# Attention over graph edges on one core: the edge networks' steps in another order, and one wait less on GpSimd

## The chip, the cores and the metric

One core of a Trainium2 chip. The number given is the device time of one execution in microseconds (us). Engines are called TensorE (PE in the profile, its weight loads PEld), VectorE (DVE), ScalarE (ACT), GpSimd (POOL) and SyncE (SP).

## The reference

A graph with 6250 nodes of 64 features and 206,250 edges sorted by their first node runs through two layers: a relation layer (gather, gate, segment sum, tanh) and an attention layer. The kernel's stages follow them; the change is in the attention layer's pass over the edges:

```python
W_k = lin(ssp(lin(edge_attr, wkn_w1, wkn_b1)), wkn_w2, wkn_b2)   # edge network, 32 -> 16 -> 16
keys_j = lin(W_k[:, None, :] * h_keys[col], wkl_w, wkl_b)        # 4 heads of 16
qk_ij = jnp.sum(queries_i * keys_j, axis=-1)
alpha = segment_softmax(qk_ij, row, n)
W_v = lin(ssp(lin(edge_attr, wvn_w1, wvn_b1)), wvn_w2, wvn_b2)   # the second edge network
msg_j = lin(W_v[:, None, :] * h_values[col], wvl_w, wvl_b)
aggr = jax.ops.segment_sum(alpha[:, :, None] * msg_j, row, num_segments=n)
```

with `ssp(x) = softplus(x) - log 2`. All of it is in float32.

## The kernel before

`attention_layer` (line 1313 on) handles the sorted edges as 128 runs, one for each partition, of 1612 edges, in 62 chunks of T = 26 edges a partition. The loop helper emits the first pair of chunks, a hardware loop over the 29 between, and the last pair; in each body b = 0, 1 is the chunk of the pair and n = 2i + b its number. Each engine has its own written-out order, and they meet at semaphores alone. A wait is passed when its semaphore has reached a count, so `wait_ge(s_w, n + 1)` is "chunk n's turned weights are there".

For one chunk n:

- SyncE loads the chunk's edge records (`attr`, line 1376) and query starts (`qin`, line 1378), two buffers each.
- VectorE's `index` writes the chunk's node numbers as integers (`idx`, line 1518) and where a new first node starts (`same`, line 1526). It stands at the head of the turn before, so `s_idx` for n comes when VectorE enters turn n - 1.
- GpSimd issues 26 indirect DMAs (line 1395), each of which gathers one row of keys and values (512 bytes) for every partition into `got[b]`. Before the first of them it waits for `s_used` (the buffer's last user, chunk n - 2), `s_idx`, and `s_w` >= n, that is for chunk n - 1's turned weights.
- The edge networks, for both `W_k` and `W_v` at once: ScalarE packs the attributes (`flat_attr`, line 1448); TensorE transposes them in 7 groups, two halves of 4 and 3, into bank `p_a` (line 1411); ScalarE copies them out (`attr_t`, line 1452); TensorE's first product goes to `p_z` (line 1416); ScalarE takes Relu and the absolute value (lines 1456 and 1457), an exponential and a logarithm (lines 1459 and 1460), which make the softplus; VectorE's `activated` adds the two parts (line 1530); TensorE's second product goes to `p_a` again (line 1420), half by half, the second after the copy of the first; ScalarE adds the bias (`net_t`, line 1467, in `networks_end`); TensorE turns the result back to edges on partitions (`p_w`, line 1424), after VectorE is through with the chunk before's (`s_value`).
- VectorE's `chunk`: a scan that carries each query along its run (line 1537, after ScalarE's `marks`, line 1442), then, with `p_w` and the gathered rows there, `prod` (line 1545), a product with the network's weights (1548), a sum by head (1549), the running maximum (1557), `drop` and `below` (1560 to 1563), the value product (1567, `s_value`); it waits for ScalarE's exponentials (lines 1472 to 1475, `s_exp`), multiplies them in (`add_a`, line 1572, `s_used`) and scans the state (line 1580, `s_state`).
- ScalarE turns the state for the store and issues it (lines 1483 and 1486).

In one turn n ScalarE does: query n+1 laid out, the whole network of chunk n+1 up to the logarithm, then `finish(n)`: exponentials of n, `networks_end(n+1)`, the copy of the maxima, then with the state there `marks(n+1)`, the copy of the state and the store. VectorE's `activated(n+1)` stands between the value product and the wait for the exponentials.

In the stage before and the ones after, other indirect DMAs run: `sort` (line 625, scatters) and `attention_nodes` (line 1696, 49 gathers in a row); their rows are used too.

Of the kernel before, what the change touches and what calls it, by code (L numbers as in the profile page):

```python
# [22 lines left out]
P = 128  # L23
# [8 lines left out]
CHUNKS = NT // T  # L32
# [4 lines left out]
G = 4  # L37
# [1275 lines left out]
def attention_layer(k):  # L1313
# [4 lines left out]
    with ExitStack() as ctx:  # L1318
# [31 lines left out]
        p_a, p_z = bank("p_a"), bank("p_z")  # L1350
# [10 lines left out]
        records_v, starts_v, sums_v = by_run(k.records), by_run(k.q_starts), by_run(k.sums1)  # L1361

        halves = ((0, 4 * P, 4), (4 * P, GROUPS * P, GROUPS - 4))

        with nc.Block() as block:
# [20 lines left out]
            def _(pool):  # L1386
                def body(i):
                    for b in range(2):
# [3 lines left out]
                        wait(pool, s_w, n)  # L1392
# [8 lines left out]
            @block.tensor  # L1401
            def _(pe):
                def body(i):
                    for b in range(2):
                        n = 2 * i + b
                        pe.wait_ge(s_flat, n + 1)
                        for j, (c0, c1, groups) in enumerate(halves):
                            wait(pe, s_at_copied, 2 * n + j)
                            wait(pe, s_net_copied, 2 * n)
                            for g in range(c0 // P, c0 // P + groups):  # L1410
                                last = nc.tensor.transpose(p_a[:, g * P - c0:(g + 1) * P - c0], flat_attr[:, g * G:(g + 1) * G, :].rearrange("p t c -> p (t c)"), k.ident[:])  # L1411
                            last.then_inc(s_at, 1)
                        for j, (c0, c1, groups) in enumerate(halves):
                            pe.wait_ge(s_at_copied, 2 * n + j + 1)
                            wait(pe, s_z_read, 2 * n + j)
                            nc.tensor.matmul(p_z[:, 0:c1 - c0], k.w1_t[:], attr_t[:, c0:c1], start=True, stop=True).then_inc(s_z, 1)
                        pe.wait_ge(s_ssp, n + 1)
                        for j, (c0, c1, groups) in enumerate(halves):
                            wait(pe, s_net_copied, 2 * n + j)
                            nc.tensor.matmul(p_a[:, 0:c1 - c0], k.w2_t[:], relu[:, c0:c1], start=True, stop=True).then_inc(s_net, 1)  # L1420
                        wait(pe, s_value, n)
                        pe.wait_ge(s_net_copied, 2 * n + 2)
                        for g in range(GROUPS):
                            last = nc.tensor.transpose(p_w[:, g * P:(g + 1) * P], net_t[:, g * P:(g + 1) * P], k.ident[:])
                        last.then_inc(s_w, 1)

                loop(pe, body)

            @block.scalar
            def _(act):  # L1430
# [13 lines left out]
                def networks(n, i, b):  # L1444
# [3 lines left out]
                    nc.scalar.copy(flat_attr[:, 0:T, :], attr[b][:, :, 0:EC]).then_inc(s_flat, 1)  # L1448
                    wait(act, s_z, 2 * n)
                    for j, (c0, c1, _) in enumerate(halves):  # L1450
                        act.wait_ge(s_at, 2 * n + j + 1)
                        nc.scalar.copy(attr_t[:, c0:c1], p_a[:, 0:c1 - c0]).then_inc(s_at_copied, 1)
                    wait(act, s_net, 2 * n)
                    for j, (c0, c1, _) in enumerate(halves):
                        act.wait_ge(s_z, 2 * n + j + 1)
                        nc.scalar.activation(relu[:, c0:c1], p_z[:, 0:c1 - c0], ACT.Relu, bias=k.b1_c[:])
                        nc.scalar.activation(soft[:, c0:c1], p_z[:, 0:c1 - c0], ACT.Abs, bias=k.b1_c[:]).then_inc(s_z_read, 1)
# [4 lines left out]
                def networks_end(n):  # L1462

                    wait(act, s_w, n)
                    for j, (c0, c1, _) in enumerate(halves):
                        act.wait_ge(s_net, 2 * n + j + 1)
                        nc.scalar.activation(net_t[:, c0:c1], p_a[:, 0:c1 - c0], ACT.Identity, bias=k.b2_c[:]).then_inc(s_net_copied, 1)

                def finish(n, i, b):
# [6 lines left out]
                    if not at_end(i, b):  # L1476
                        networks_end(n + 1)
# [513 lines left out]
```

## Time and profile before

| | |
|---|---|
| median of 3 runs | 5864.14 us (5855.48 to 5867.09) |
| the profiled execution | 5865.56 us |
| its span | 5863.7 us |
| attention layer's loop, first to last `prod` | 3436.7 to 5692.3 us |
| GpSimd, VectorE, ScalarE, TensorE busy over the span | 56%, 66%, 47%, 46% |

The page gives for each engine its busy time and share of the span, then 40 slices, the DMA queues, the chain that ended last, and groups of instructions by line. The order of time (timeline) has for each instruction its start, its length, and in brackets how long the engine had stood still before it and what ended that. "issue" there means that the engine waited for nothing that the profile shows, "remote" that a semaphore came whose sender isn't resolved. Ends of TensorE's matmuls are modelled; starts are records.

### The profile page before, as it was taken

The page shows a single profiled execution, that of the slowest core. Times are in us where ns is not written, and L with a number is a line of the kernel's source. Part 1 is how long each engine was busy: PE and PEld are TensorE (multiplying, and loading weights), DVE is VectorE, ACT ScalarE, POOL GpSimd, SP SyncE. Part 2 cuts the span into 40 slices and gives each one's busy share as a digit, 9 for nine tenths or more (in the row PEclk, how much of TensorE's full clock was granted, in tenths as well). Part 3 has the DMA queues.
Part 4 walks back from the last instruction along what each step waited for, and adds up shares of the span by engine and source line. Part 5 has one row for each costly group of instructions (what it writes and reads, how often), then busy time and mean ns, then how long its engine had stood idle before and what let it go on. Part 6 is the DMA issues. An engine that isn't in the chain of part 4 may idle for free. (4 is left out here: it accounts for less than half of the span.)

```text
span 5863.7 us, 79660 instructions
## 1 busy us (share of the span) xinstructions
PE 2726.4 (46%) x21110; PEld 1693.1 (29%) x21111; DVE 3881.4 (66%) x8751; ACT 2758.0 (47%) x5413; POOL 3278.9 (56%) x3388
## 2 busy tenths in 40 slices
PE   7655555555555555555488622322223222222223
PEld 7433333333333333333388511111111111111102
DVE  9867777777777777776599645655556666655552
ACT  3244444444444444444122345655555555555552
POOL 0146565666666565656610266666666666666653
PEclk8555555555555555555577755555555555555555
DMA  5112121212121212121477533433334343433321
GB/s 64 55 54 71 63 71 62 71 63 71 63 71 63 71 63 71 63 71 58 103 160 145 72 103 100 124 110 108 108 103 111 109 110 103 110 108 109 109 79 24
DMA packets 691304, 505.28 MB, mean 86 GB/s; under 512 B 588446, under 2 KB 605214, under 8 KB 691109
## 3 DMA queue, kind: packets, MB, share of 16 engines
q1 hardware_dynamic: 573012, 246.99, 18.2%
q0 software_dynamic: 108736, 196.93, 11.6%
q10 hardware_dynamic: 9360, 59.56, 2.7%
q14 instruction: 172, 1.40, 0.1%
q8 instruction: 24, 0.39, 0.0%
HBM read 289.96 MB, written 213.26 MB: 86 GB/s over the span
## 5 line engine op out<-in xcount | busy, mean ns | idle before, releaser
L625 POOL DMA_INDIRECT records<-rec,place x1612 | 1557.2, 966 | 1306.9 <-issue 451.0
L1395 POOL DMA_INDIRECT got_a<-kv_table,idx_a x1612 | 1539.5, 955 | 762.8 <-issue 691.9
L860 DVE SCALAR_TENSOR_TENSOR same_before<-p_src,src_f,before 128x128 bf16<-128x128 f32 x1612 | 775.0, 535 | 0.0
L711 ACT ACTIVATE lo_away<-p_lo,minus_number 128x512 bf16<-128x512 f32 x434 | 291.2, 671 | 615.5 <-remote 593.6
L668 PE MATMUL p_src<-fields,select 3*128 3x512 bf16 x434 | 248.3, 572 | 687.7 <-DVE same_before L860 512.0
L1411 PE MATMUL p_a<-ident,flat_attr 128*128 128x128 f32 x434 | 123.5, 433 | 930.5 <-issue 447.4
L807 DVE TENSOR_TENSOR picked<-p_look,hi_hot 128x392 f32<-128x392 f32 x434 | 231.5, 533 | 407.5 <-remote 398.2
L1420 PE MATMUL p_a<-relu,w_t 128*128 128x512 f32 x248 | 230.8, 1034 | 463.4 <-issue 332.5
L850 DVE TENSOR_SCALAR dst_hot<-p_dst,number 128x512 bf16<-128x512 f32 x434 | 307.3, 708 | 191.1 <-remote 178.1
L643 PE MATMUL p_look<-table_low,lo_hot_t 128*128 128x98 bf16 x1612 | 410.2, 281 | 0.0
L643 PE MATMUL p_look<-table_rest,lo_hot_t 128*128 128x98 bf16 x1612 | 409.4, 280 | 0.0
L1545 DVE TENSOR_TENSOR prod<-got_a,wide 128x1664 f32<-128x1664 f32 x62 | 117.0, 1888 | 440.2 <-remote 216.3
L643 PE MATMUL p_look<-table,lo_hot_t 128*128 128x98 bf16 x1612 | 402.3, 278 | 0.0
L730 ACT ACTIVATE h_gated<-p_h,gate_s 128x64 f32<-128x64 f32 x1586 | 372.1, 315 | 51.5 <-remote 12.2
L653 PE MATMUL p_h<-window,dst_hot 128*128 128x64 bf16 x4836 | 357.6, 242 | 65.1 <-issue 64.9
L1014 PE MATMUL acc<-high,lo_r 128*128 128x64 bf16 x1708 | 345.4, 244 | 60.0 <-DVE low L1079 40.7
L708 ACT COPY table<-p_place 128x49 f32<-128x49 f32 x434 | 91.7, 211 | 597.0 <-issue 371.6
L1411 PEld LDWEIGHTS p_a<-ident,flat_attr 128*128 128x128 f32 x434 | 75.6, 215 | 978.3 <-issue 824.4
L1014 PE MATMUL acc<-rest_r,lo_r 128*128 128x64 bf16 x1708 | 344.3, 243 | 0.0
L1014 PE MATMUL acc<-low,lo_r 128*128 128x64 bf16 x1708 | 344.2, 243 | 0.0
L653 PEld LDWEIGHTS p_h<-window,dst_hot 128*128 128x128 bf16 x4836 | 312.2, 133 | 54.2 <-issue 53.8
L1014 PEld LDWEIGHTS acc<-high,lo_r 128*128 128x128 bf16 x1708 | 291.3, 171 | 67.6 <-issue 66.3
(377 smaller groups left out, 8443.3 us busy)
## 6 DMA issues: line engine op xcount, KB each, us to landing
sums<-packed_a ACTq DMA_DIRECT2D x62, 936.0 KB
q_starts<-zero_q SPq DMA_DIRECT2D x62, 884.0 KB
rec_r<-records SPq DMA_DIRECT2D x124, 442.0 KB
qin<-q_starts SPq DMA_DIRECT2D x62, 884.0 KB
attr_a<-records SPq DMA_DIRECT2D x62, 442.0 KB
records<-rec,place POOLq DMA_INDIRECT x1612
got_a<-kv_table,idx_a POOLq DMA_INDIRECT x1612
stage<-in_edge_attr SPq DMA_DIRECT2D x61, 416.0 KB
```

Of the source, the lines that this page charges most:

```text
L625: nc.gpsimd.indirect_dma_start(k.records, bass.IndirectOffsetOnAxis(ap=place[b][:, t:t + 1], axis=0), rec[b][:, t, :], None).then_inc(s_se ...
L643: last = nc.tensor.matmul(p_look[qb][:, j * 2 * HI:(j + 1) * 2 * HI], lo_hot_t[qb][:, j * P:(j + 1) * P], part, start=(e == 0), stop=(e == 2))
L653: last = nc.tensor.matmul(p_h[qb][:, j * D:(j + 1) * D], dst_hot[qb][:, j * P:(j + 1) * P], part, start=(e == 0), stop=(e == 2))
L668: nc.tensor.matmul(p_src[:, 0:m * P], k.select[:, NODE, :], rows, start=True, stop=True).then_inc(s_src, 1)
L711: nc.scalar.activation(lo_away[qb][:, 0:m * P], p_lo[:, 0:m * P], ACT.Abs, bias=k.minus_number[:]).then_inc(s_lo_away, 1)
L730: last = nc.scalar.activation(to, p_h[qb][:, j * D:(j + 1) * D], ACT.Copy, scale=gate[b][:, t:t + 1])
L807: v.tensor_tensor(picked[:, 0:n, :, :], p_look[gb][:, 0:n * 2 * HI].rearrange("p (g a h) -> p g a h", a=2, h=HI), bc(group_hot(k, b, g, HI ...
L850: v.tensor_scalar(dst_hot[qb][:, 0:m * P], p_dst[:, 0:m * P], k.number[:], None, ALU.is_equal).then_inc(s_dst_hot, 1)
L860: last = v.scalar_tensor_tensor(same_before[:, first:first + j + 1, :].rearrange("p g e -> p (g e)"), p_src[:, 0:(j + 1) * P], k.src_f[:, ...
L1014: last = nc.tensor.matmul(acc[:, to(t // SUPER)], lo[b][:, :, t], part, start=False, stop=True, skip_group_check=True)
L1395: nc.gpsimd.indirect_dma_start(got[b][:, t, :], None, k.kv_table, bass.IndirectOffsetOnAxis(ap=idx[b][:, t:t + 1], axis=0)).then_inc(s_got ...
L1420: nc.tensor.matmul(p_a[:, 0:c1 - c0], k.w2_t[:], relu[:, c0:c1], start=True, stop=True).then_inc(s_net, 1)
```

## The change

Only `attention_layer` is touched.

- GpSimd: the wait for `s_w` goes; `s_used` and `s_idx` stay.
- PSUM: instead of `p_a` (transposed attributes, second product) and `p_z` (first product) there are `p_n[0]` and `p_n[1]`, one for each half, used by all three in turn.
- TensorE, in turn n: second product of chunk n+1, transposes of chunk n+2, turned weights of n+1, first product of n+2.
- ScalarE, in turn n: lay out the query n+1, `networks_end(n+1)`, `flattened(n+2)`, exponentials of n, `attributes(n+2)`; then with the state of n there `marks(n+1)`, `activation(n+2)`, the maxima's and the state's copies, the store.
- VectorE: `activated(n+1)` moves ahead, between the query scan and `prod` of turn n, and is made of seven additions of 128 columns, one for each group, instead of one of 896.
- Before the loop, networks 0 and 1 are begun.

```diff
-        p_a, p_z = bank("p_a"), bank("p_z")
+        p_n = [bank(f"p_n{j}") for j in range(2)]
...
+        def follows(i, b, more):
+
+            return not (isinstance(i, int) and 2 * i + b + more >= CHUNKS)
...
                         wait(pool, s_used, n - 1)
                         pool.wait_ge(s_idx, n + 1)
-                        wait(pool, s_w, n)
                         pool.sem_inc(k.s_passed, 1)
...
+                def attributes(m):
+                    pe.wait_ge(s_flat, m + 1)
+                    wait(pe, s_net_copied, 2 * m)
+                    for j, (c0, c1, groups) in enumerate(halves):
+                        for g in range(c0 // P, c0 // P + groups):
+                            last = nc.tensor.transpose(p_n[j][:, g * P - c0:(g + 1) * P - c0], flat_attr[:, g * G:(g + 1) * G, :].rearrange("p t c -> p (t c)"), k.ident[:])
+                        last.then_inc(s_at, 1)
+
+                def first_product(m):
+                    for j, (c0, c1, groups) in enumerate(halves):
+                        pe.wait_ge(s_at_copied, 2 * m + j + 1)
+                        nc.tensor.matmul(p_n[j][:, 0:c1 - c0], k.w1_t[:], attr_t[:, c0:c1], start=True, stop=True).then_inc(s_z, 1)
+
+                def second_product(m):
+                    for j, (c0, c1, groups) in enumerate(halves):
+                        pe.wait_ge(s_ssp, 2 * m + j + 1)
+                        pe.wait_ge(s_z_read, 2 * m + j + 1)
+                        nc.tensor.matmul(p_n[j][:, 0:c1 - c0], k.w2_t[:], relu[:, c0:c1], start=True, stop=True).then_inc(s_net, 1)
+
+                def turned(m):
+                    wait(pe, s_value, m)
+                    pe.wait_ge(s_net_copied, 2 * m + 2)
+                    for g in range(GROUPS):
+                        last = nc.tensor.transpose(p_w[:, g * P:(g + 1) * P], net_t[:, g * P:(g + 1) * P], k.ident[:])
+                    last.then_inc(s_w, 1)
+
+                attributes(0)
+                first_product(0)
+                second_product(0)
+                attributes(1)
+                turned(0)
+                first_product(1)
+
                 def body(i):
                     for b in range(2):
                         n = 2 * i + b
...
+                        if follows(i, b, 1):
+                            second_product(n + 1)
+                        if follows(i, b, 2):
+                            attributes(n + 2)
+                        if follows(i, b, 1):
+                            turned(n + 1)
+                        if follows(i, b, 2):
+                            first_product(n + 2)
...
-                def finish(n, i, b):
+                def exponentials(n):
 
                     act.wait_ge(s_below, n + 1)
                     nc.scalar.activation(add[:, D:QW, 1:T1], below[:], ACT.Exp)
                     nc.scalar.activation(weight, below[:], ACT.Exp)
                     nc.scalar.activation(factor[:, 0:D, :].rearrange("p (h d) t -> p h d t", h=NH), bc(drop[:], 2, HD), ACT.Exp)
                     nc.scalar.activation(factor[:, D:QW, :], drop[:], ACT.Exp).then_inc(s_exp, 1)
-                    if not at_end(i, b):
-                        networks_end(n + 1)
+
+                def finish(n, i, b):
+
+                    act.wait_ge(s_state, n + 1)
+                    if follows(i, b, 1):
+                        marks(n + 1, i + b, 1 - b)
+                    if follows(i, b, 2):
+                        activation(n + 2)
                     wait(act, s_store[b], 16 * i)
                     c.mark(nc.scalar.copy(packed[b][:, :, QW:SW], top[b][:, :, 1:T1].rearrange("p h t -> p t h")))
-                    act.wait_ge(s_state, n + 1)
-                    if not at_end(i, b):
-                        marks(n + 1, i + b, 1 - b)
...
-                        if not at_end(i, b):
+                        if follows(i, b, 1):
                             lay_out(n + 1, i + b, 1 - b)
-                            networks(n + 1, i + b, 1 - b)
+                            networks_end(n + 1)
+                        if follows(i, b, 2):
+                            flattened(n + 2, i + 1, b)
+                        exponentials(n)
+                        if follows(i, b, 2):
+                            attributes(n + 2)
                         finish(n, i, b)
...
                 def activated(n):
                     dve.wait_ge(s_soft, n + 1)
-                    nc.vector.tensor_tensor(relu[:], relu[:], soft[:], ALU.add).then_inc(s_ssp, 1)
+                    for j, (c0, c1, groups) in enumerate(halves):
+                        for g in range(groups):
+                            at = slice(c0 + g * P, c0 + (g + 1) * P)
+                            last = nc.vector.tensor_tensor(relu[:, at], relu[:, at], soft[:, at], ALU.add)
+                        last.then_inc(s_ssp, 1)
...
                     c.then(nc.vector.tensor_copy(query[1 - b][:, :, 0:1], factor[:, :, T:T1]))
 
+                    if follows(i, b, 1):
+                        activated(n + 1)
                     dve.wait_ge(s_w, n + 1)
                     dve.wait_ge(s_got[b], SCATTERED * (i + 1))
```

## Rows read from the trace of the kernel before

**Rows 1.** The page, busy us, share of the span and instructions by engine

```profile
PE 2726.4 (46%) x21110; PEld 1693.1 (29%) x21111; DVE 3881.4 (66%) x8751; ACT 2758.0 (47%) x5413; POOL 3278.9 (56%) x3388
```

**Rows 2.** The source line 1545: durations in ns (least, median, most), first and last start

```profile
L1545 DVE TENSOR_TENSOR prod<-got_a,wide x62: 1886/1887/1890, 3436.7 to 5692.3; 128x1664 f32<-128x1664 f32 x62
```

**Rows 3.** Busy time by stretch: window, us, PE, PEld, DVE, ACT, POOL, clock, DMA

```profile
3450.00:5600.00 2150.00, 629.54 (x1282) 269.01 (x1282) 1281.49 (x1220) 1223.97 (x1232) 1438.76 (x1507) 0.50 0.39 108
```

**Rows 4.** Groups by line, 3450 to 5600 us: busy us, mean ns, idle before

```profile
L1395 POOL DMA_INDIRECT got_a<-kv_table,idx_a x1507 | 1439.2, 955 | 711.5 <-issue 660.8 <-remote 34.0 <-DVE idx_a L1518 16.7
L1537 DVE TENSOR_TENSOR_SCAN wide<-wide,query 128x1836 f32<-128x1836 f32 x58 | 231.4, 3990 | 50.6 <-issue 43.4 <-ACT wide L1442 7.3
...
L1474 ACT ACTIVATE wide<-drop 128x1728 f32<-128x1728 f32 x59 | 96.3, 1633 | 0.0
L1442 ACT COPY wide<-same 128x1768 f32<-128x1768 f32 x58 | 94.9, 1636 | 216.7 <-DVE state_a L1580 216.7
...
L1472 ACT ACT_TABLE_LOAD x59 | 75.7, 1283 | 1.0
```

**Rows 5.** Order of time, 4500 to 4625 us: start, length, instruction, idle before

```profile
4506.47 1.92 PE L1416 MATMUL p_z<-attr_t,w_t 128*128 128x512 f32 x2
...
4511.83 0.69 ACT L1456 ACTIVATE relu<-p_z,b_c 128x512 f32<-128x512 f32 x1 [4.63 <-issue]
...
4521.11 1.09 DVE L1530 TENSOR_TENSOR relu<-relu,soft 128x896 f32<-128x896 f32 x1 [3.74 <-ACT soft L1460]
4521.54 1.47 POOL L1395 DMA_INDIRECT got_a<-kv_table,idx_a  x1 [0.30 <-issue]
...
4528.67 1.73 PE L1424 MATMUL p_w<-ident,net_t 128*128 128x128 f32 x7 [1.78 <-issue]
...
4532.35 0.18 DVE L1518 CAST idx_a<-attr_a 128x26 int32<-128x26 f32 x1 [0.61 <-DVE state_a L1580]
...
4537.07 0.95 POOL L1395 DMA_INDIRECT got_a<-kv_table,idx_a  x1 [0.30 <-issue]
...
4542.42 1.09 PE L1411 MATMUL p_a<-ident,flat_attr 128*128 128x128 f32 x4 [12.03 <-ACT flat_attr L1448]
...
4546.28 0.59 ACT L1452 COPY attr_t<-p_a 128x512 f32<-128x512 f32 x1 [4.10 <-remote]
4546.37 1.89 DVE L1545 TENSOR_TENSOR prod<-got_a,wide 128x1664 f32<-128x1664 f32 x1 [8.47 <-remote]
...
4546.95 0.95 POOL L1395 DMA_INDIRECT got_a<-kv_table,idx_a  x1 [8.93 <-issue]
...
4553.61 0.27 DVE L1563 TENSOR_TENSOR below_a<-logit_carry,top 128x104 f32<-128x104 f32 x1
...
4560.61 2.99 DVE L1572 TENSOR_TENSOR add_a<-got_a,wide 128x1664 f32<-128x1664 f32 x1 [2.42 <-issue]
...
4563.65 1.73 PE L1424 MATMUL p_w<-ident,net_t 128*128 128x128 f32 x7 [0.77 <-ACT net_t L1467]
...
4621.07 0.94 POOL L1395 DMA_INDIRECT got_a<-kv_table,idx_a  x1 [8.89 <-issue]
```

**Rows 6.** Order of time in the last stage, 5733 to 5806 us

```profile
5733.21 0.96 POOL L1696 DMA_INDIRECT sums_f<-sums,last_at  x1 [2.04 <-DMA sums<-fixed,fix_to]
...
5756.31 0.69 DVE L1843 TENSOR_TENSOR xs<-xs,out_br 128x512 f32<-128x512 f32 x1 [8.91 <-remote]
...
5773.77 2.08 PE L1719 MATMUL p_of<-out_t,feat_f 128*128 128x128 f32 x8 [5.31 <-issue]
...
5794.18 0.94 POOL L1696 DMA_INDIRECT sums_f<-sums,last_at  x1 [0.30 <-issue]
...
5801.86 0.69 DVE L1843 TENSOR_TENSOR xs<-xs,out_br 128x512 f32<-128x512 f32 x1 [40.06 <-remote]
```

**Rows 7.** Order of time in the first stage's sort, 343 to 349 us

```profile
343.25 0.96 POOL L625 DMA_INDIRECT records<-rec,place  x1 [0.30 <-issue]
...
348.40 0.57 DVE L807 TENSOR_TENSOR picked<-p_look,hi_hot 128x392 f32<-128x392 f32 x1 [23.92 <-remote]
```

More of the change, by code:

```diff
@@ L1405, in body @@
                         n = 2 * i + b
[L1406 to L1425, printed above, removed]
+                        if follows(i, b, 1):
[6 more added lines that the diff above has]
+                            first_product(n + 2)
                 loop(pe, body)
@@ L1442, in marks, with flattened @@
                     nc.scalar.copy(factor[:, :, 1:T1], bc(same[b][:], 1, QW)).then_inc(s_keep, 1)
-                def networks(n, i, b):
+                def flattened(n, i, b):
                     act.wait_ge(s_rec[b], 16 * (i + 1))
@@ L1448, in networks, with attributes @@
                     nc.scalar.copy(flat_attr[:, 0:T, :], attr[b][:, :, 0:EC]).then_inc(s_flat, 1)
+                def attributes(n):
                     wait(act, s_z, 2 * n)
@@ L1451, in networks, with activation @@
                         act.wait_ge(s_at, 2 * n + j + 1)
-                        nc.scalar.copy(attr_t[:, c0:c1], p_a[:, 0:c1 - c0]).then_inc(s_at_copied, 1)
+                        nc.scalar.copy(attr_t[:, c0:c1], p_n[j][:, 0:c1 - c0]).then_inc(s_at_copied, 1)
+                def activation(n):
                     wait(act, s_net, 2 * n)
@@ L1466, in networks_end @@
                         act.wait_ge(s_net, 2 * n + j + 1)
-                        nc.scalar.activation(net_t[:, c0:c1], p_a[:, 0:c1 - c0], ACT.Identity, bias=k.b2_c[:]).then_inc(s_net_copied, 1)
-                def finish(n, i, b):
+                        nc.scalar.activation(net_t[:, c0:c1], p_n[j][:, 0:c1 - c0], ACT.Identity, bias=k.b2_c[:]).then_inc(s_net_copied, 1)
+                def exponentials(n):
                     act.wait_ge(s_below, n + 1)
@@ L1491, in _ @@
                 lay_out(0, 0, 0)
-                networks(0, 0, 0)
+                flattened(0, 0, 0)
+                attributes(0)
+                activation(0)
                 networks_end(0)
+                flattened(1, 0, 1)
+                attributes(1)
+                activation(1)
                 def body(i):
@@ L1567, in chunk @@
                     nc.vector.tensor_tensor(by_head, by_head, bc(nets[:, :, HD:EC], 2, NH), ALU.mult).then_inc(s_value, 1)
-                    if not at_end(i, b):
-                        activated(n + 1)
                     dve.wait_ge(s_exp, n + 1)
```

4 lines of the change are left out of this document (2 added, 2 removed).

## The prediction, made before the change was built or run

> **What bounds the kernel now.** I read the totals of engines first [rows 1]: no engine is busy more than 66% of the span, so the limit has to be looked for by stage. The stage that the change touches is the attention layer; its first and last `prod` lie at 3436.7 and 5692.3 us [rows 2], that is 2255.6 us for 61 steps, 36.98 us a chunk. In the stretch 3450 to 5600 GpSimd is busiest with 67%, VectorE has 60%, ScalarE 57% [rows 3]. By lines [rows 4], GpSimd does one thing there, the indirect DMA of line 1395, 955 ns each; the row "0.30 <-issue" behind most of them in the order of time [rows 5] says that back to back they start every 1.25 us, so 26 take 32.5 us. GpSimd therefore stands still 4.5 us a chunk, and it does so in one piece: [rows 5] shows the gap of 8.93 us that ends at 4546.95 and the next one, of 8.89 us, that ends at 4621.07. 74.12 us apart, two chunks: 2 x 32.5 + 8.9 + some tenths. That gap is what the stage is over GpSimd's own time.
>
> What ends it? Burst n waits for `s_used`, `s_idx` and `s_w` >= n (the turned weights of chunk n-1). Before the gap ending at 4546.95, the index was written at 4532.35 + 0.18, and the seven transposes of line 1424 are modelled as ended at 4528.67 + 1.73 = 4530.4. The last indirect DMA started at 4537.07. Still nothing moved until 4546.3: then ScalarE's copy of `p_a` ("<-remote"), VectorE's `prod` and GpSimd's next burst all started within 0.7 us, although the copy waits only for transposes modelled as ended at 4543.51 [rows 5]. What the three have in common is TensorE. So I read it so: TensorE's completions came late, at about 4546.2, 15.8 us after the modelled end and 8.2 us after GpSimd's last issue ended (4538.0). In the other chunk of each pair the transposes at 4563.65 held nobody up. The page shows the same twice elsewhere. In the last stage GpSimd issues 49 indirect DMAs in a row from 5733.21 to 5795.1; products modelled as ended at 5775.85 are followed by VectorE only at 5801.86, 26 us later and 6.7 us after the last issue ended; earlier in that run VectorE had waited 8.91 us until 5756.31 for the same kind of product ("remote") [rows 6]. In the first stage VectorE waits 23.92 us for `p_look`, until 348.40, which is 4.2 us after a run of 26 ended at 344.2 [rows 7]. 26, 49 and 52 issues in a row, and a release 4.2, 6.7 and 8.2 us after the last: about 0.16 us for each issue. Early in a run (1 to 27 in this stage) completions come on time; `p_z` of 4506.47 + 1.92 at about the 28th issue is read at 4511.83, 3.4 us late [rows 5]. The Trainium skill ("Perfetto Trace Analysis", Tensor Engine Instruction) says that the profiler's end of a TensorE instruction is computed and not observed, and that the semaphore comes when PSUM acknowledges; the trace agrees (26 us between the two above).
>
> **The change, part by part.** (1) *No `s_w` wait on GpSimd*: 62 waits less. GpSimd is then stopped only by `s_used` (chunk n-2) and `s_idx` n, both written when VectorE enters turn n-1. That wait was what stopped GpSimd while TensorE's completion was outstanding, and its stop was what let the completion through. The gap of 8.9 us per pair goes if nothing else stops GpSimd.
> (2) *Networks up to two chunks ahead*: the same transposes, products and activations are issued, in another order. `turned(n+1)` now follows the value product of chunk n, some 9.3 us after `prod` began (4546.37 to the end of `below` at 4553.88, and then one product of 1.9 us), so it has some 23 us until `prod` n+1 instead of none; `attributes`, `first_product` and `second_product` have 6 to 13 us each before ScalarE blocks on them. This absorbs the 1 to 5 us of lateness at issues 28 to 44, not 15 and more. The queue behind them: ScalarE's `networks_end(n+1)` waits for the second product and stands in front of `exponentials(n)`; VectorE's `add_a`, its state scan, and with them `s_used` and the next index, wait behind that.
> (3) *A bank for each half*: the wait of the second product for the first copy (0.9 us, hidden) goes: 0.
> (4) *Exponentials at once*: `below` ends at 4553.61 + 0.27, `add_a` starts at 4560.61 because line 1460 and its table load stood in front [rows 5]. Now a table load (1.28 us) and 2.2 us of exponentials (1.63 the widest, three small ones [rows 4]): `add_a` 3.2 to 4.5 us earlier. VectorE's turn becomes prod to state 17 to 18.3 us, marks 1.7, scan and copy 4.4 [rows 4], `activated` 1.1 to 2, some 26 us, under GpSimd's 32.5. No gain of its own.
> (5) *Seven adds of 128 for one of 896*: 1.09 us becomes at most 7 x 0.27 = 1.9 (the 128x104 operations take 0.27 [rows 5]), hidden by (4). GpSimd's issue at 4521.54 took 1.47 instead of 0.95 beside this add [rows 5]; were each chunk's stretch saved, 62 x 0.5 = 31 us at most, 0 at least; about 12 if one in two and a half. Only counted where GpSimd bounds.
> (6) *Record and query loads, the store*: the record load of chunk n+2 is released by VectorE's `same` of chunk n and is read over 30 us later; a load is there some 5 us after its issue. On SP's and ScalarE's queues nothing new blocks: 0. The second network before the loop costs ScalarE some 9 us, behind the 32 us of the first burst: 0 to 3.
>
> **The sum.** What is decisive is what TensorE's completions do when GpSimd is not stopped for them. Taking from [rows 5, 6, 7] that after some 45 issues in a row a completion waits until GpSimd stops: VectorE and ScalarE go on until `networks_end` lacks its product; by then the indices of two further bursts are written, so GpSimd issues three bursts, 97.5 us, before it stops. Release: between 8.2 us (as now) and 0.16 x 78 = 12.5 us after. Then `networks_end` 1.2, `flattened` 0.9, table 1.3, exponentials 2.2, `add_a` 3.0, copy 0.2, scan 4.0, index 0.8 = 13.6 us until the next burst. 119.3 to 123.6 us for three chunks, 39.8 to 41.2 a chunk; I take 40.5. Against 36.98 that is +3.5 x 59 chunks (the first and last two run freer) = +207. If the held step is `first_product`, 13 us of activation and `activated` come in addition: 45 a chunk, +480. 5865.56 (span 5863.7 and 1.9 around it) + 207 = 6072; the profiled run lies 1.4 over the median, so 6071.
>
> **Rivals.** *GpSimd runs free* (0.26): completions late by a few us only, inside the new slack. For it: issues 1 to 44, where the lateness is 0 to 5 us, and in the last stage one completion came at the 19th issue without a stop. Then 32.6 to 32.8 a chunk, 4.3 less x 61 = -262: 5603. The Trainium skill ("SBUF — State Buffer", SBUF: two separate sides) says that only VectorE and GpSimd share a port and that TensorE never waits on anyone at SBUF; by it this rival would be the forecast, and [rows 6, 7] speak against it.
> *Partly held* (0.12): completions trickle through at 5 to 10 us each, and the slack takes most of it: 34 to 36 a chunk, 5685 to 5805.
> *The hidden queue fills* (0.08): 52 issues and 8.2 us of draining are 1.41 us an issue; if GpSimd is slowed to that, 26 take 36.7 us, 0.3 x 61 less than now: 5847. Half of it, with some late completions, falls within the 0.2% (12 us, about what a measurement of this kernel can tell from no change).
> *The change doesn't do what it says* is in the second: if ScalarE's blocked waits keep the networks from running ahead.
>
> **Chances.** Forecast (held until GpSimd stops) 0.54; 5603: 0.26; 5685 to 5805: 0.12; 5847: 0.08. Slower by over 0.2% 0.54, within 0.2% 0.05, faster 0.41. The forecast's own range is 5990 to 6300. The range reaches from the free case, 5595, to 6300; above it lies part of the 45 us case.
>
> **What would show it.** Right: GpSimd in runs of 78 issues or more, gaps of 20 us and over between them, ended by index or `add_a`; ScalarE's line of `networks_end` or `attributes` waiting 15 us and more for TensorE. Wrong: GpSimd without a gap over 1 us for many chunks and `prod` every 32.6 us. Exponentials right behind `below` confirm (4), and no issue over 1.1 us beside the adds (5). Wrong by size if runs end after 52 because VectorE is blocked a chunk earlier.

## The result and the profile after

The changed kernel takes 6196.84 us (median of 4 runs, 6185.89 to 6204.86) against 5863.1 (4 runs, 5855.48 to 5867.09) of the kernel before: a ratio of 1.057, interval 1.0553 to 1.0586. Forecast were 6071, range 5595 to 6300.

The page of the changed kernel, busy time by engine over a span of 6184.1 us (against [rows 1]):

```profile
PE 2660.0 (43%) x21110; PEld 1717.2 (28%) x21111; DVE 3904.3 (63%) x9123; ACT 2736.3 (44%) x5413; POOL 3259.4 (53%) x3388
```

Every engine is busy for as long as before, within 2.5%, and all shares fell: the 320.4 us by which the span grew are waiting. The source lines of the product by factor (`prod`) and of GpSimd's gathers (durations in ns: least, median, most; then first and last start), against [rows 2, 4]:

```profile
L1594 DVE TENSOR_TENSOR prod<-got_a,wide x62: 1872/1880/1889, 3436.1 to 6012.9; 128x1664 f32<-128x1664 f32 x62
...
L1398 POOL DMA_INDIRECT got_a<-kv_table,idx_a x1612: 938/944/1092, 3393.9 to 6005.2; - x180
...
  DVE idx_a L1561: 607.0, 29
  issue: 491.2, 1578
```

The first product starts where it did (3436.1, before 3436.7), the last one 171.2 us before the end of the span (before 171.4). Between them lie 2576.8 us, 42.24 a chunk against 36.98 [rows 2]; 5.26 x 61 = 321 us, which is the whole loss. GpSimd waits 607 us for the index, in 29 waits, 20 of them over 25 us long; [rows 4] had 16.7 us of that kind. Counted from the starts of its issues, it falls into a cycle of exactly three chunks: 52 issues, a break of 0.9 to 1.7 us, 26 issues, then nothing for close to 30 us, and that every 127.6 us, 42.5 a chunk. The waits of one stretch, 3450 to 5900 us (engine, line and what it waited for: us, times, longest):

```profile
ACT relu L1486 <- remote: 694.1, 72, 22.5
DVE relu L1576 <- ACT soft L1490: 659.0, 42, 28.8
POOL got_a L1398 <- DVE idx_a L1561: 565.8, 27, 29.7
```

They are one chain: ScalarE waits for TensorE, VectorE for ScalarE, GpSimd for VectorE. One instance of it in the order of time, 4345 to 4410 us (against [rows 5]):

```profile
4345.50 2.07 PE L1417 MATMUL p_n<-attr_t,w_t 128*128 128x512 f32 x2 [6.29 <-issue]
...
4353.29 0.48 ACT L1479 COPY attr_t<-p_n 128x384 f32<-128x384 f32 x1 [7.84 <-remote]
...
4353.82 1.65 PE L1417 MATMUL p_n<-attr_t,w_t 128*128 128x384 f32 x2 [6.24 <-issue]
...
4377.14 0.69 ACT L1486 ACTIVATE relu<-p_n,b_c 128x512 f32<-128x512 f32 x1 [21.84 <-remote]
...
4377.91 0.94 POOL L1398 DMA_INDIRECT got_a<-kv_table,idx_a  x1 [0.30 <-issue]
4379.16 0.94 POOL L1398 DMA_INDIRECT got_a<-kv_table,idx_a  x1 [0.30 <-issue]
...
4383.39 0.58 ACT L1486 ACTIVATE relu<-p_n,b_c 128x384 f32<-128x384 f32 x1 [4.98 <-remote]
...
4387.80 1.50 DVE L1576 TENSOR_TENSOR relu<-relu,soft 128x128 f32<-128x128 f32 x7 [28.08 <-ACT soft L1490]
...
4389.23 1.88 DVE L1594 TENSOR_TENSOR prod<-got_a,wide 128x1664 f32<-128x1664 f32 x1
...
4401.44 3.00 DVE L1619 TENSOR_TENSOR add_a<-got_a,wide 128x1664 f32<-128x1664 f32 x1 [2.92 <-ACT wide L1505]
...
4404.61 3.98 DVE L1627 TENSOR_TENSOR_SCAN state_a<-wide,add_a 128x1836 f32<-128x1836 f32 x1
...
4408.80 0.18 DVE L1561 CAST idx_a<-attr_a 128x26 int32<-128x26 f32 x1 [0.20 <-DVE state_a L1627]
...
4409.76 0.94 POOL L1398 DMA_INDIRECT got_a<-kv_table,idx_a  x1 [29.66 <-DVE idx_a L1561]
```

The two halves of the first product are modelled as ended at 4347.57 and 4355.47. ScalarE gets the first at 4377.14 and the second at 4383.39, 29.6 and 27.9 us later; the second comes 3.3 us after GpSimd's 78th issue has ended (4380.10). From there 26.4 us of dependent work lead to GpSimd's next issue.

The first half came at 4377.14 while GpSimd was still issuing (its next issues start at 4377.91 and 4379.16), and this is the rule in this trace, not the exception. I set each recorded increment of a semaphore by TensorE against the modelled end of the instruction that made it. Between 3450 and 5900 us, 328 of 401 left a record; 146 of them came more than 2 us late, the latest 33.0 us, and 124 of these 146 came in the middle of a run of issues. The late ones come in the order in which they were made; 94 times two of them follow each other inside a run, 40 times 4.9 us apart and never less. What was made while GpSimd stood still mostly came at once in this trace: 4 of 136 were over 2 us late, against 142 of the 192 made during a run. In the kernel before (3450 to 5600 us), 66 of 258 came more than 2 us late, up to 16.5 us, and 47 of these 66 after the run.

### The profile page after: what moved, and what is told of

Same layout as the page of the kernel before. It is cut to its first block and busy times, and to the rows that moved or that the text cites. A ratio compares the mean times of both kernels' runs of the same rounds, so it can differ in the third digit from the quotient of the medians.

```text
span 6184.1 us, 79942 instructions
## 1 busy us (share of the span) xinstructions
PE 2660.0 (43%) x21110; PEld 1717.2 (28%) x21111; DVE 3904.3 (63%) x9123; ACT 2736.3 (44%) x5413; POOL 3259.4 (53%) x3388
## 5 line engine op out<-in xcount | busy, mean ns | idle before, releaser
L1398 POOL DMA_INDIRECT got_a<-kv_table,idx_a x1612 | 1524.1, 945 | 1099.7 <-DVE idx_a L1561 607.0
L1423 PE MATMUL p_n<-relu,w_t 128*128 128x512 f32 x248 | 207.4, 992 | 1380.3 <-DVE relu L1576 844.3
L1576 DVE TENSOR_TENSOR relu<-relu,soft 128x128 f32<-128x128 f32 x434 | 93.6, 286 | 853.0 <-ACT soft L1490 734.2
L1423 PEld LDWEIGHTS p_n<-relu,w_t 128*128 128x128 f32 x248 | 72.9, 324 | 1507.4 <-DVE relu L1576 901.3
L1486 ACT ACTIVATE relu<-p_n,b_c 128x512 f32<-128x512 f32 x124 | 78.4, 633 | 758.2 <-remote 739.3
L1584 DVE TENSOR_TENSOR_SCAN wide<-wide,query 128x1836 f32<-128x1836 f32 x62 | 247.4, 3990 | 186.7 <-issue 162.2
```

The costliest lines, as they stand in the source:

```text
L1398: nc.gpsimd.indirect_dma_start(got[b][:, t, :], None, k.kv_table, bass.IndirectOffsetOnAxis(ap=idx[b][:, t:t + 1], axis=0)).then_inc(s_got ...
L1423: nc.tensor.matmul(p_n[j][:, 0:c1 - c0], k.w2_t[:], relu[:, c0:c1], start=True, stop=True).then_inc(s_net, 1)
L1584: nc.vector.tensor_tensor_scan(flat, flat, query[b][:].rearrange("p c t -> p (c t)"), 0.0, ALU.mult, ALU.add).then_inc(s_q, 1)
```

## The experiments

Four groups of runs landed on four chips. The kernel before was timed on each again, and it isn't the same there: 5868.03 us on the chip of E1 to E4, 5028.36 (E5 to E8), 5026.85 (E9, E10) and 5027.06 (E12; one run of 5025.04 beside E11). I call the first a chip that holds TensorE's results, that is, on which the other engines get them late, and the others chips that don't; the traces below show the difference, not its reason. Whether it belongs to the chip or to its condition at the time was not tested. The expectations of E5 to E8 were written for a chip that holds.

### On the chip that holds

**E1**: the old order without GpSimd's wait for the turned weights.

```diff
                         pool.wait_ge(s_idx, n + 1)
-                        wait(pool, s_w, n)
                         pool.sem_inc(k.s_passed, 1)
```

> The kernel before with one line taken out: GpSimd no longer waits for the turned weights. Order of the networks, banks and exponentials are those of before. Theory held (TensorE's completions are held up while GpSimd issues indirect DMAs without a stop): runs of 78 issues; the turned weights of every third chunk are modelled as ended at about the 47th issue and are read only when the run of 78 is over; cycle 97.5 + 3.3 + 22 = 123 us for three chunks, 41.0 a chunk, 5863 + 4.0 x 59 = 6100 us (6040 to 6160). Rival order (the new order of steps is what costs, the wait on GpSimd was harmless): no slower than 5870, and down to 5600 if GpSimd was only being paced for nothing.

Measured: 6137.45 us, ratio 1.0464 (1.0391 to 1.0537). Product by factor, and GpSimd's line:

```profile
L1544 DVE TENSOR_TENSOR prod<-got_a,wide x62: 1886/1887/1890, 3454.2 to 5945.9; 128x1664 f32<-128x1664 f32 x62
...
L1394 POOL DMA_INDIRECT got_a<-kv_table,idx_a x1612: 938/944/1859, 3417.1 to 5914.6; - x180
...
  issue: 487.4, 1585
  DVE idx_a L1517: 472.5, 27
```

2491.7 / 61 = 40.85 us a chunk, with runs of 78 and of 52 and 26 issues. So the removed wait alone does most of the damage, in the old order too: 3.87 of the 5.26 us a chunk.

**E2**: the changed kernel with another wait for GpSimd in that place.

```diff
                         pool.wait_ge(s_idx, n + 1)
+                        pool.wait_ge(s_z, 2 * n + 2)
                         pool.sem_inc(k.s_passed, 1)
```

> The changed kernel with one wait added: before burst n GpSimd waits for both halves of the first product of chunk n (s_z), the step that is read 28 to 30 us late in the changed kernel. Theory held: GpSimd stops after 52 issues at most while a completion is outstanding, is released some 3 to 8 us later, and the time falls by most of the loss: 36 to 38.5 us a chunk, 5800 to 5960 us. Rival order (ScalarE's and VectorE's new order costs by itself): GpSimd wasn't the cause, an added wait can't help, 6190 us or more.

Measured: 5869.16 us, ratio 1.0011 (0.9976 to 1.0045):

```profile
L1595 DVE TENSOR_TENSOR prod<-got_a,wide x62: 1872/1880/1889, 3490.4 to 5722.5; 128x1664 f32<-128x1664 f32 x62
...
L1399 POOL DMA_INDIRECT got_a<-kv_table,idx_a x1612: 939/945/1092, 3454.0 to 5719.9; - x180
...
  issue: 472.7, 1551
  remote: 259.6, 41
```

2232.1 / 61 = 36.59 us a chunk: GpSimd stops every 26 or 52 issues, for 3.3 to 8.7 us (twice for 1.1), and the whole loss of pitch is gone (42.24 to 36.59; before 36.98). TensorE's results still come late (3500 to 5700 us: 161 of 303 by more than 2 us), but at most by 25.7 us, and GpSimd now stops for the ones it waits for. The stage starts late, though, since burst 0 now waits for network 0: GpSimd at 3454.0 instead of 3393.9, the first `prod` at 3490.4 instead of 3436.1 us. These 54 us eat up the 0.39 x 61 = 24 us that the pitch gains on the kernel before, which leaves the profiled execution (span 5893.1) 29 us longer than the kernel before's; it is one of the longer ones, and by medians the two are the same.

**E3 and E4**: the 26 gathers of a chunk become one plain DMA of GpSimd, in the new order and in the old one. The gather by node is left out, the bytes stay; the waits for the gathered rows count one DMA in place of 26.

```diff
-                        for t in range(T):
-                            nc.gpsimd.indirect_dma_start(
-                                got[b][:, t, :], None, k.kv_table,
-                                bass.IndirectOffsetOnAxis(ap=idx[b][:, t:t + 1], axis=0)).then_inc(s_got[b], 16)
+                        nc.gpsimd.dma_start(got[b][:], k.kv_table[bass.ds(i * 2 * T + b * T, P * T), :].rearrange("(p t) c -> p t c", t=T)).then_inc(s_got[b], 16)
```

> The changed kernel with the 26 gathers of a chunk replaced by one plain DMA of as many bytes from the same table, issued by GpSimd behind the same waits (the gathered rows are the wrong ones: the gather by node is left out; everything else is computed). Theory held: no run of issues, so no held completion; VectorE's turn of 26 to 29 us sets the pace, 27.5 a chunk: 6190 - 15 x 61 = 5275 us (5180 to 5400). Rival order: the pace stays at 37 us a chunk or over, 5860 us or more. Rival transfers (the gathered bytes, not the issues, hold TensorE up): late completions as before, 5800 to 6190.

> The same replacement in the kernel before (the gather by node is left out there too). Theory held: VectorE's turn with prod to state 21.4 us, marks 1.8, scan 4.3, index 1 sets the pace, if TensorE's chain is in time: 29 to 33 us a chunk, 5390 to 5620 us, slower than the changed order by 1 to 4 us a chunk, since the exponentials come later there. Rival order: faster than the changed order by 3 us a chunk or more.

Measured: E3 5329.67 us (ratio 0.9086, 0.9018 to 0.9155), E4 5633.63 (0.9605, 0.954 to 0.967). The product by factor of E3, then of E4:

```profile
L1591 DVE TENSOR_TENSOR prod<-got_a,wide x62: 1874/1879/1889, 3494.6 to 5181.1; 128x1664 f32<-128x1664 f32 x62
```

```profile
L1542 DVE TENSOR_TENSOR prod<-got_a,wide x62: 1886/1889/1889, 3454.5 to 5479.1; 128x1664 f32<-128x1664 f32 x62
```

27.65 us a chunk in the new order, 33.19 in the old. Without a run of issues nothing is held: on this same chip none of 418 recorded increments (E3, 3500 to 5150 us) and none of 409 (E4, 3500 to 5450 us) came later than 0.02 us after the modelled end. The bytes gathered for a chunk are the same and come in less time, so the bytes alone don't hold TensorE; the 26 issues, or their smaller packets (4096 bytes against 13,312), do. The new order is then 5.5 us a chunk the better one. So the order itself isn't slow; it is slow beside unbroken runs of issues. E4's time lies 14 us over the range expected for it, and the difference between the orders over the 1 to 4 us expected.

### On chips that don't hold

**E8**: the changed kernel with the removed wait put back (`wait(pool, s_w, n)`, the line that E1 takes out).

> The changed kernel with the wait that the change took from GpSimd put back: chunk n's issues wait for chunk n - 1's turned weights. In the new order those are made a chunk earlier, before chunk n - 2's products by factor, so the wait is met before GpSimd comes to it. Theory (the stop counts, not the wait as such): runs of 78 issues stay, 42 us per chunk, 6150 to 6210 us. Rival (taking the wait away was the whole damage, and with it back the new order is worth its 5.5 us per chunk or at least nothing lost): 5600 to 5870 us.

Measured: 4994.78 us against 5028.36, ratio 0.9934 (0.9917 to 0.9951). On this chip the premise of both expectations is missing. Product by factor and GpSimd's line:

```profile
L1595 DVE TENSOR_TENSOR prod<-got_a,wide x62: 1879/1888/1889, 2874.7 to 4859.9; 128x1664 f32<-128x1664 f32 x62
...
L1399 POOL DMA_INDIRECT got_a<-kv_table,idx_a x1612: 941/947/1085, 2839.5 to 4857.2; - x180
...
  issue: 487.5, 1599
  DVE idx_a L1562: 15.1, 13
```

GpSimd makes all 1612 issues without a break as long as 1 us, 32.54 us a chunk, and TensorE's results are read at once all the same. In the order of time:

```profile
4007.75 3.35 PE L1424 MATMUL p_n<-relu,w_t 128*128 128x512 f32 x4 [11.59 <-DVE relu L1577]
...
4015.09 1.89 DVE L1595 TENSOR_TENSOR prod<-got_a,wide 128x1664 f32<-128x1664 f32 x1 [6.79 <-DMA got_a<-kv_table,idx_a]
...
4022.24 0.27 DVE L1613 TENSOR_TENSOR below_a<-logit_carry,top 128x104 f32<-128x104 f32 x1
...
4022.54 0.29 ACT L1503 ACTIVATE add_a<-below_a 128x104 f32<-128x104 f32 x1 [4.78 <-DVE below_a L1613]
...
4024.77 3.02 DVE L1620 TENSOR_TENSOR add_a<-got_a,wide 128x1664 f32<-128x1664 f32 x1 [0.47 <-ACT wide L1506]
...
4028.21 3.98 DVE L1628 TENSOR_TENSOR_SCAN state_a<-wide,add_a 128x1836 f32<-128x1836 f32 x1
```

Everybody is ahead of GpSimd here, and VectorE waits for its data. By the same count of TensorE's increments as above, in E8, 2900 to 4800 us, none of 410 came more than 0.02 us late, and the same is true of every other trace of these three chips (E5 to E7 and E9 to E12, 401 to 408 increments each). The restored wait never stopped GpSimd in E8 (no row names `p_w`), so E8 stands for the changed kernel on this chip; the changed kernel itself was not timed on such a chip.

**E5**: the wait of E2, but only from chunk 2 on.

```diff
                         pool.wait_ge(s_idx, n + 1)
+                        if not at_start(i):
+                            pool.wait_ge(s_z, 2 * n + 2)
                         pool.sem_inc(k.s_passed, 1)
```

> The changed kernel with GpSimd waiting for chunk n's first products before chunk n's 26 issues, but only from chunk 2 on, so that the first two chunks' issues start as in the changed kernel (3393.9 us) and not 60 us later. The order of the networks is whole. Theory (long runs of issues hold TensorE's results back; a short stop lets them through): 36.6 us per chunk as with the wait from chunk 0 on, first product by factor near 3440 instead of 3490.4, so 5869 - 50 = 5820 us (5800 to 5850), which is below both kernels. Rival (the start is worth nothing, since chunk 2 then waits for what the start gained): 5860 to 5880.

Measured: 4995.37 us, ratio 0.9934 (0.9918 to 0.9951), 32.53 us a chunk. The wait costs nothing that can be seen where nothing is held (E8, with the other wait, has 32.54). What it gives on a holding chip stays an expectation (5820), made of E2's pitch and the changed kernel's start.

**E6 and E9**: a pause behind each chunk's issues that depends on nobody.

```diff
                         pool.wait_ge(s_idx, n + 1)
+                        wait(pool, s_pause, n)
                         pool.sem_inc(k.s_passed, 1)
...
                                 bass.IndirectOffsetOnAxis(ap=idx[b][:, t:t + 1], axis=0)).then_inc(s_got[b], 16)
+                        nc.gpsimd.memset(idle[:], 0.0).then_inc(s_pause, 1)
```

> The changed kernel with a memset of 4096 columns of a tile that nobody reads behind each chunk's 26 issues, and GpSimd waiting for its end before the next chunk's issues: from the 128-column and the one-column memsets of this trace (194 and 99 to 106 ns) an estimate of 3.1 us. The pause depends on nothing that another engine does; nothing that is computed changes. Theory (the run of issues as such holds TensorE's results, any stop of a few us lets them through): runs of 26 issues, 32.5 + 3.3 = 35.8 us per chunk, 3620 + 61 x 35.8 = 5804 us (5780 to 5860). Rival A (the wait on s_z helps because it orders GpSimd behind the networks, not because it stops it; a stop of its own gives nothing): 42.2 us per chunk or more, 6150 to 6300. Rival B (3 us is too short a stop): in between, 38 to 41 us per chunk, 5940 to 6120.

> The kernel of e6 once more (a memset of 4096 columns behind each chunk's 26 issues), on whatever chip it lands: on the chip of e5 to e8 nothing held TensorE's results back, and e6 could only show what the pause costs there, 36.5 us per chunk. If the kernel before takes about 5865 us on this chip (a chip that holds): the theory (the run of issues holds the results, and any stop lets them through) says 36.5 us per chunk, 3620 + 61 x 36.5 = 5846 us (5820 to 5890), with runs of 26; the rival (a stop of its own gives nothing, it has to be a wait on TensorE) says 6150 to 6400. If the kernel before takes about 5030 us, this is the run of e6 again: 5230 to 5245.

Measured: 5240.38 us (ratio 1.0422, 1.0404 to 1.0439) and 5237.21 (1.0418, 1.0401 to 1.0435). The memset took 3.53 us (estimated 3.1), the pitch is (5098.6 - 2871.9) / 61 = 36.50 us:

```profile
L1404 POOL MEMSET idle<- x62: 3525/3530/3539, 2868.7 to 5096.9; 128x4096 f32 x62
```

These show only the price of a stop where nothing is held: 4.0 us a chunk, one for one, so GpSimd is the bound there. Whether a stop of its own would free TensorE on a holding chip stays open.

**E7 and E10**: the same issues with 272 bytes a partition in place of 512, keys and values left out; the buffers are cleared once before the loop.

```diff
-                                got[b][:, t, :], None, k.kv_table,
+                                got[b][:, t, 0:QW], None, k.q_table,
```

> The changed kernel with the same 1612 issues in the same order, but each fetches 68 columns of the query table (272 bytes per partition) and not 128 of keys and values (512); the other 60 columns of the buffer are zero. Keys and values are left out of what is computed. It tells the issues from the bytes that they move. Theory (the issues hold TensorE's results): runs of 78 issues with stops near 29 us as in the changed kernel, 41.5 to 42.5 us per chunk, 6150 to 6210 us. Rival (the transferred bytes or the load on the DMA engines do it): the hold is gone or much shorter, 33 to 38 us per chunk, 5650 to 5950 us.

> The kernel of e7 once more (1612 issues of 272 bytes per partition in place of 512; keys and values left out). If this chip holds (kernel before about 5865 us): the theory (the issues do it, not the bytes) says runs of 78 issues and 41.5 to 42.5 us per chunk, 6150 to 6210 us; the rival (bytes do it) 33 to 38 us per chunk, 5650 to 5950. If it doesn't hold: 4985 to 5000 as in e7.

Measured: 4993.88 and 4990.06 us (ratios 0.9934, 0.9918 to 0.9951, and 0.9928, 0.9911 to 0.9944), 32.49 us a chunk in E7: halving the bytes gives 0.05 us a chunk against E8, so there it is the issue itself that costs 1.25 us. What the bytes of each issue add to the hold stays open for the same reason; E3 shows only that as many bytes without the issues don't hold.

**E11**: the kernel before, unchanged, for its trace.

> The kernel before, unchanged, for its profile on whatever chip this is. On a chip that doesn't hold TensorE's results back (about 5028 us): GpSimd's 26 issues per chunk are 32.5 us without a stop, so the theory (there GpSimd's issues are the bound of both kernels) expects 61 chunks at 32.5 to 33.2 us by the product by factor, and GpSimd stopped only by short waits for the turned weights, 0 to 0.7 us per chunk; the 33 us by which the changed order was faster there is then either those stops (0.5 us per chunk) or the start and the end of the stage. Rival: VectorE's chain is the bound there too, with GpSimd idle several us per chunk. On a chip that holds (about 5865 us): 36.9 us per chunk as in its first profile.

Measured: 5024.07 us. Product by factor, gathers and the wide add:

```profile
L1545 DVE TENSOR_TENSOR prod<-got_a,wide x62: 1886/1887/1890, 2872.4 to 4890.2; 128x1664 f32<-128x1664 f32 x62
...
L1395 POOL DMA_INDIRECT got_a<-kv_table,idx_a x1612: 940/944/1853, 2835.3 to 4887.6; - x180
...
  issue: 489.4, 1606
  DVE idx_a L1518: 12.5, 4
  PE p_w L1424: 0.6, 2
```

33.08 us a chunk, and the wait for `p_w` costs 0.6 us in all: the short stops that I expected aren't there either. What differs from E8 is the most in the durations, 1853 against 1085 ns. 58 of the 1612 issues take over 1.1 us, 39.2 us more than 58 median ones, and each of them overlaps line 1530, such as this one:

```profile
2913.66 1.08 DVE L1530 TENSOR_TENSOR relu<-relu,soft 128x896 f32<-128x896 f32 x1
2913.70 1.85 POOL L1395 DMA_INDIRECT got_a<-kv_table,idx_a  x1 [0.30 <-issue]
```

GpSimd's stage is 2053.2 us long, in E8 2018.6: 34.6 us, and the times differ by 29 to 34. In the first profile of the kernel before, on a holding chip, only 26 issues are stretched, by 13.7 us.

**E12**: E5's kernel with one wide add again.

```diff
-                    for j, (c0, c1, groups) in enumerate(halves):
-                        for g in range(groups):
-                            at = slice(c0 + g * P, c0 + (g + 1) * P)
-                            last = nc.vector.tensor_tensor(relu[:, at], relu[:, at], soft[:, at], ALU.add)
-                        last.then_inc(s_ssp, 1)
+                    nc.vector.tensor_tensor(relu[:], relu[:], soft[:], ALU.add).then_inc(s_ssp, 2)
```

> The kernel of e5 (the changed kernel with GpSimd waiting for chunk n's first products from chunk 2 on) with one 896-wide add in place of the seven 128-wide ones, as before the change; nothing that is computed changes. On a chip that doesn't hold TensorE's results (kernel before about 5027 us) the theory, that the wide add, both of whose operands lie in SBUF, stretches the one issue of GpSimd that it meets by 0.68 us (39.2 us over 58 issues in e11, none in e5 and e8), expects some 58 issues over 1.1 us, GpSimd's stage 34 to 39 us longer than the 2016.7 us of e5, and 4995 + 34 = 5029 us (5020 to 5036); the rival (they come from something else in the order before, such as the transposes or the exponentials) expects no issue over 1.1 us and 4990 to 5000. On a chip that holds them (about 5865): e5's expectation of 5820 us plus 0 to 36, 5820 to 5856, with the first product by factor near 3440; 5865 or more would say that the start is worth nothing.

Measured: 5024.68 us (5004.03 to 5028.02), ratio 0.998 (0.9967 to 0.9994):

```profile
L1592 DVE TENSOR_TENSOR prod<-got_a,wide x62: 1886/1886/1889, 2870.9 to 4892.7; 128x1664 f32<-128x1664 f32 x62
...
L1400 POOL DMA_INDIRECT got_a<-kv_table,idx_a x1612: 940/944/1792, 2836.3 to 4890.1; - x180
```

60 issues are stretched again, by 42.2 us, GpSimd's stage is 2054.8 us long and the pitch 33.14. So in the traced execution (5026.93 us) the wide add costs what the changed order gains on such a chip. Of the ten executions, six took 5023.55 to 5028.02 us and four 5004.03 to 5007.14; no trace of one of the four is kept, so some 20 us of the gain aren't explained for them.

## Why the prediction came out as it did

The direction and the cycle of three bursts came as forecast; the loss was 334 us by medians where 207 were forecast, and the mechanism was right in one half. The range from 5595 to 6300 took in both the free and the held case, so that the time lies inside it says little; that it lies in the forecast's own 5990 to 6300 says more.

**What bounds the kernel** was read rightly for the measured chip in this: while GpSimd issues without a break, TensorE's results are late (without the runs of issues, 0 late of 418 and 409 in E3 and E4), and taking away its stop costs more than the stop: without it, in the old order, the pitch is 40.85 (E1), and with another stop in the new order 36.59 (E2). Wrong was the step "a completion waits until GpSimd stops". In the changed kernel 124 of the 146 late ones came while it was issuing, one after another; in the cycle above the second half came 6.3 us after the first, as in 19 cycles of the stretch, though GpSimd had stopped 3.3 us before it, and the ones that follow each other inside a run are mostly 4.9 us apart. The forecast took its rule from the kernel before, where 47 of 66 did come after the run. The rival "partly held", that completions trickle through at 5 to 10 us each, is nearer to what the trace shows; its price of 34 to 36 us a chunk is not, since delays of up to 33 us were far over the slack.

**(1) The wait** carries most of the loss, as forecast. E1 gives 3.87 us a chunk for it alone.

**(2) Two chunks ahead** buys slack of 6 to 13 us and meets results that are 28 to 30 us late; the forecast held that it wouldn't absorb 15. Three bursts to a cycle came as forecast. Wrong was which step is held: the sum was made for `networks_end` lacking the second product, and it was `activation` lacking the first. That case stood in the text as "+13 us, 45 a chunk", but it was not the one taken. Two sizes in it:

| of one cycle, three chunks, us | forecast | measured |
|---|---|---|
| three bursts | 97.5 | 97.9 with the break |
| last issue's end to the held result | 8.2 to 12.5 | 3.3 |
| result to GpSimd's next issue | 13.6 (26.6 with the first product held) | 26.4 |
| a chunk | 39.8 to 41.2, taken 40.5 (45) | 42.5; 42.24 over 61 |

The tail was 13 us longer and the release 5 to 9 us shorter, and the two errors partly cancelled: that the time came out as near as it did is in part luck. The rule "0.16 us for each issue before it", drawn from releases at 4.2, 6.7 and 8.2 us [rows 5, 6, 7], does not hold: after 78 issues the result came at 3.3 us, and the half before it at 4377.14, inside the run. The count was wrong in a second way too: the forecast put the excess on 59 chunks and counted 3.5 us each; it was 5.26 on 61.

**(3) A bank for each half**: no row of the changed kernel's chain names it; it was not taken out by itself.

**(4) Exponentials at once**: `add_a` starts 4.7 us after `below` (4396.73 to 4401.44) where it was 6.7 before, 2.0 us earlier instead of 3.2 to 4.5, because `networks_end` and `flattened` (1.16 and 0.89 us) and the table load stood ahead in ScalarE's queue; the product to the state's end took 19.4 us instead of 17 to 18.3. Where nothing is held (E8) both are as forecast: 2.3 us behind `below`, 4.4 earlier, and 17.1 us. In either case it doesn't shorten the stage by itself, as forecast.

**(5) Seven adds** take 1.50 us (at most 1.9 forecast), and no issue is over 1.092 us. The saving was bounded at 0 to 31 us and called countable only where GpSimd bounds: on the chips where it does, it is 34 us by E8 against E11 (0.68 us for each of 58 stretched issues in place of the 0.5 forecast), with the reservation made at E12; on the measured one it is drowned by the waiting. The Trainium skill ("SBUF — State Buffer", SBUF: two separate sides) says that VectorE with two SBUF inputs and a GpSimd instruction that reads SBUF lock each other out of a shared port. The trace agrees for the wide add: the issue at 2913.70 takes 1.85 us instead of 0.94, and the add ends 1.04 us after that issue's start. That seven adds of the same operands leave the issues under 1.1 us is the runs' own finding.

**(6)** The first product at 3436.1 and the unchanged 171 us behind the last one confirm 0.

**The rival "GpSimd runs free"**, at 32.6 to 32.8 us a chunk, is what happens in the new order where nothing is held (32.54 in E8, 32.53 in E5). Its pitch was right, its mechanism and its gain were not: completions aren't a few us late inside the new slack there, they aren't late at all, and in E11 the kernel before runs free there too, so the gain is 34 us and not 262. So the change costs 5.7% where TensorE's results are held and gains 0.7% where they aren't (by E8, which stands for it there), and the trace of before, taken where they are, could tell only the first.

**Where the kernel before spends 841 us more on a holding chip** (5863.7 against 5022.2 of span in E11): 564.3 us ahead of the first product by factor, mostly in the sort, whose line 625 waits there for TensorE and "remote"; 237.8 in the attention loop; 39.4 behind it. The sort's line in the kernel before, on the holding chip and then in E11:

```profile
L625 POOL DMA_INDIRECT records<-rec,place x1612: 956/962/1217, 233.4 to 2866.3; - x180
...
  issue: 451.0, 1375
  PE p_dst L670: 282.1, 128
  remote: 270.3, 104
```

```profile
L625 POOL DMA_INDIRECT records<-rec,place x1612: 954/958/1211, 232.8 to 2304.5; - x180
...
  issue: 469.0, 1538
  ACT rec L736: 229.6, 1
  ACTq L762: 27.2, 1
  PE p_dst L670: 24.0, 70
```

**Open**: why TensorE's semaphores come late beside a run of issues, why only on one of the four chips of the experiments, and whether any pause, or fewer bytes in each issue, would help there. On the holding chip no run that keeps the gathers beat both kernels; E5's is the candidate, and it costs nothing on the others.

## What to carry to other kernels

A wait that looks like a mere dependency can be what makes an engine stop, and the stop can be what others live on: before removing one, look at what starts in the moment when it stops. Time both orders on more than one chip when the trace shows results that come long after their modelled end, since the sign of a change can hang on that. And look at when each late result comes, all through the trace: a few cases at the ends of runs suggested a rule here that the counts don't bear out. Beside GpSimd issuing indirect DMAs without a break, try splitting wide VectorE operations on two SBUF operands: seven short ones cost 0.4 us more here and took 0.68 us off the issue that each wide one met.

## What the runs showed of the hardware

- On the chip of E1 to E4, and wherever the result was measured, TensorE's semaphore increments came up to 33.0 us after the modelled end (146 of 328 over 2 us) while GpSimd issued 52 to 78 indirect DMAs in a row, and none came late there with one plain DMA a chunk in their place (0 of 418 and 409 over 0.02 us). On three others GpSimd made 1612 issues in a row, and none of the increments came late (0 of 410 in E8). The same kernel takes 5864 and 5027 us.
- Most held results of the changed kernel came inside a run of issues (124 of 146; for example 4377.14, two issues before the last), in the order in which they were made and at least 4.9 us apart inside a run; in E2 some came 0.7 us apart. The length of the run alone doesn't set the delay.
- An indirect DMA of 128 rows starts every 1.25 us, with 272 bytes a row as with 512.
- A 128x896 add of two SBUF operands lengthens the one issue it meets by 0.68 us on average (39.2 / 58); beside seven 128x128 adds no issue took more than 1.1 us (E5, E8).
